# Turning the first query tile's probabilities by a DMA transpose in an attention and FFN kernel, with a reordered opening and finish

## What is computed

```python
q = rope((LN(x) @ Wq) as 32 heads of 64)
k = rope((LN(x) @ Wk) as 8 heads of 64), repeated 4 times
v = (LN(x) @ Wv) as 8 heads of 64, repeated 4 times
p = softmax(causal(q @ k.T / 8))
x = x + (p @ v) @ Wo
scale = max(absmax(LN(x)), 1e-7) / 127            # per token
xq = clip(round(LN(x) / scale), -128, 127)
x = x + float16((xq @ weight.T) * scale * w_scale + bias)
```

## Time and profile before

| | |
|---|---|
| median of three runs | 805.92 us |
| the profiled execution, its own time | 809.36 us |
| span of the profile of that execution | 807.5 us |
| PE busy | 762.0 us (94%), 8230 matmuls |
| DVE busy | 631.9 us (78%) |
| ACT busy | 627.7 us (78%) |
| POOL busy | 572.4 us (71%) |
| hardware DMA queue, share of the 16 DMA engines | 42.5% |
| chain that ended last | PE 73%, DVE 8%, ACT 5%, issue 5%, SPq 4%, DMA 4% |

### The profile page before, as it was taken

How to read it: one execution, slowest core, us unless ns; L and a number is a source line. 1 busy time by engine, 2 the same in 40 slices (tenths; PEclk the granted TensorE clock), 3 DMA queues, 4 the chain that set the end, 5 groups by cost and what they waited for, 6 DMA issues and landing times.

```text
span 807.5 us, 23412 instructions
## 1 busy us (share of the span) xinstructions
PE 762.0 (94%) x8230; PEld 641.1 (79%) x8230; DVE 631.9 (78%) x1392; ACT 627.7 (78%) x1731; POOL 572.4 (71%) x526
## 2 busy tenths in 40 slices
PE   3899999999999999999999999999999999999993
PEld 2678888888888887788888888888888887888771
DVE  5757877787878887777778888878788787887886
ACT  4488888788877887788778878888788777887772
POOL 4466877777777886877886887877786887676403
PEclk9799999999999999999999999999999999999995
DMA  8254545564554554554544454455544455354300
GB/s 263 53 124 91 132 112 139 126 153 99 133 125 99 125 122 93 122 117 108 135 114 112 100 127 112 112 125 120 125 106 116 110 117 128 80 119 100 86 2 26
DMA packets 56994, 90.99 MB, mean 113 GB/s; under 512 B 12592, under 2 KB 19248, under 8 KB 56880
## 3 DMA queue, kind: packets, MB, share of 16 engines
q1 hardware_dynamic: 53808, 79.02, 42.5%
q0 software_dynamic: 3072, 10.49, 4.9%
HBM read 16.06 MB, written 2.10 MB: 22 GB/s over the span
## 4 chain that ended last, share of the span: by engine, by line
PE 73%; DVE 8%; ACT 5%; issue 5%; SPq 4%; DMA 4%; POOL 0%; ACTq 0%; POOLq 0%; DVEq 0%
PE x_bank L623 21%; PE t_bank L735 15%; PE o_bank L751 11%; PE s_bank L719 9%; PE s_bank L720 8%; PE s_bank L722 3%; DMA qT<-wv 3%; PE ot_bank L802 3%; ACT prob L1030 2%; PE t_bank L623 2%; DVE probT L1353 2%; SPq L304 2%; SPq L338 1%; DVE o_norm L1388 1%; SPq L342 1%
## 5 line engine op out<-in xcount | busy, mean ns | idle before, releaser
L1030 ACT ACTIVATE prob<-s_bank,neg_max 128x384 f32<-128x384 f32 (+3 forms) x512 | 266.5, 531 | 62.9 <-DVE neg_max L1364 62.8
L1364 DVE TENSOR_REDUCE neg_max<-s_bank 128x1 f32<-128x384 f32 (+3 forms) x352 | 215.9, 636 | 58.3 <-PE s_bank L722 55.5
L1353 DVE SCALAR_TENSOR_TENSOR probT<-t_bank,probT 128x512 f16<-128x512 f32 x320 | 215.5, 682 | 29.5 <-ACT probT L1042 28.7
L1042 ACT ACTIVATE probT<-t_bank 128x512 f16<-128x512 f32 x320 | 189.2, 600 | 43.3 <-PE t_bank L735 38.7
L735 PE MATMUL t_bank<-ident,prob 128*128 128x128 f32 x1280 | 199.1, 278 | 5.0 <-DVE probT L1353 1.4
L719 PE MATMUL s_bank<-kT,qT 128*128 128x384 f32 (+3 forms) x512 | 178.2, 363 | 5.4 <-DMA qT<-wv 3.0
L492 POOL TENSOR_TENSOR wv<-raw,wv 128x512 fp32r<-128x512 f32 x62 | 79.6, 1284 | 132.2 <-ACT wv L991 132.2
L720 PE MATMUL s_bank<-kT,qT 128*128 128x384 f32 (+3 forms) x512 | 157.1, 322 | 0.0
L735 PEld LDWEIGHTS t_bank<-ident,prob 128*128 128x128 f32 x1280 | 137.6, 141 | 14.8 <-ACT prob L1030 7.3
L751 PE MATMUL o_bank<-value,probT 128*128 128x64 f16 x3840 | 138.4, 193 | 0.0
L751 PEld LDWEIGHTS o_bank<-value,probT 128*128 128x128 f16 x3840 | 131.4, 98 | 6.0
(11 more groups left out here) (123 smaller groups left out, 954.4 us busy)
## 6 DMA issues: line engine op xcount, KB each, us to landing
qT<-wv SPq DMA_DIRECT2D x248, 128.0 KB, 2.4
swp<-raw SPq DMA_DIRECT2D x320, 64.0 KB, 2.0
kT<-key_pair SPq DMA_DIRECT2D x128, 128.0 KB, 2.4
wg_raw<-in_w_group POOLq DMA_DIRECT2D x16, 384.0 KB, 4.8
wg_raw<-in_w_group POOLq DMA_DIRECT2D x16, 256.0 KB, 3.8
resid<-in_x SPq DMA_DIRECT2D x4, 512.0 KB, 8.7
out<-resid SPq DMA_DIRECT2D x16, 128.0 KB, 2.1
wo_stage<-in_w_out SPq DMA_DIRECT2D x4, 256.0 KB, 3.0
```

Source lines behind the costliest of these rows:

```text
L1030: nc.scalar.activation(prob[:, slot:slot + blocks, h, :], s_bank[G % SCORE_BANKS][:, at * n:(at + 1) * n].rearrange("p (k n) -> p k n", n= ...
L1042: nc.scalar.activation(turned_half[B % TURNED][HI], t_bank[B % TURN_BANKS][:, :], ACT.Copy, scale=PROB_SCALE).then_inc(probT_hi, 1)
L1353: nc.vector.scalar_tensor_tensor(out=turned_half[B % TURNED][LO], in0=t_bank[B % TURN_BANKS][:, :], scalar=PROB_SCALE, in1=turned_half[B % ...
L1364: nc.vector.tensor_reduce(neg_max[:, s % 2, u:u + len(heads)], s_bank[G % SCORE_BANKS][:, 0:len(heads) * n].rearrange("p (h n) -> p h n", ...
```

## The change

**The first query tile.** `turn(s, 0)` is gone from PE. ACT now makes the high part directly from `prob` into a new tensor `parts` (128 partitions, two parts of 4 x 128 columns in 16 bits), and DVE makes the low part from `prob` and `parts`, both in SBUF. SP then issues one DMA transpose of `parts` into `probT` (`turn_first_block`), and `attend(s, 0)` waits for that transfer. It moves from behind `turn(s, 1)` to behind `scores(s, 7)`. The split now stands at the end of the loop body before: on ACT right behind the exponentials of the first query tile, on DVE right behind `maxima(s + 1, 2)` and ahead of `add_product(s, 2)`. `invert_sums(s, 0)` and `normalise_output(s, 0)` move behind `maxima(s, 7)`. `pe_turn_no` numbers the nine turns that stay.

**Weight stage.** The output weight has one staging buffer in place of two. One chunk is loaded, rounded and subtracted in every step up to the eighth, in place of two in every second.

**Opening.** PE projects the second step's first queries ahead of `values(0)`, and `values(0)` to `values(2)` stand ahead of `turn_xn(4)`. ACT rounds the second group weight in place of POOL. DVE makes the low parts of the value weight ahead of the second batch's statistics, and `cast_ffn_weights` moves to the opening's end.

**Finish.** `normalise_output` of the last step's query tile 3 moves ahead of that step's `add_product(s, 2)`. The last four token tiles are normalised in two pairs (0 and 1, 2 and 3) in place of three and one, and tile `LOOP_TILES + 2` is normalised by ACT in place of POOL.

```diff
-WO_STAGES = 2
+WO_STAGES = 1
...
+        parts = sb("parts", [P, 2, GROUP_HEADS * P], f16)
...
+            def turn_first_block(s):
+                B = block_no(s, 0)
+                sp.wait_ge(probT_lo, B + 1)
+                if B >= TURNED:
+                    sp.wait_ge(pv_done, B - TURNED + 1)
+                sp.dma_start_transpose(probT[B % TURNED][:, :, :, :].rearrange("p a h n -> p (a h) n"),
+                                       parts[:, :, :].rearrange("p a n -> p (a n)")).then_inc(first_turned, 16)
+
             for s in range(STEPS):
+                turn_first_block(s)
                 swap_key_halves(s + 2)
...
-                if s % 2 == 0:
-                    load_wo(s + 2)
-                    load_wo(s + 3)
+                load_wo(s + 2)
...
             def attend(s, t):
...
-                pe.wait_ge(probT_lo, B + 1)
+                if t == 0:
+                    pe.wait_ge(first_turned, 16 * s + 16)
+                else:
+                    pe.wait_ge(probT_lo, B + 1)
...
             project(0, 0)
             project(0, 1)
             project_keys(0)
+            project(1, 0)
             values(0)
+            values(1)
+            values(2)
+            spread_power()
             turn_xn(4)
-            values(1)
-            spread_power()
...
             for s in range(STEPS + 1):
-                turn(s, 0)
                 scores(s, 4)
...
                 turn(s, 1)
-                attend(s, 0)
                 turn(s, 2)
                 out_product(s - 1, 3)
                 turn_quant(done_tile(s))
                 scores(s, 7)
+                attend(s, 0)
...
             def keep_probT(s, t):
...
+                if t == 0:
+                    act.wait_ge(exp_done, unit_no(s, 0, GROUP_HEADS))
+                    if s:
+                        act.wait_ge(first_turned, 16 * s)
+                    nc.scalar.activation(parts[:, HI, :], prob[:, B % PROBS, :, :].rearrange("p h n -> p (h n)"), ACT.Copy,
+                                         scale=PROB_SCALE).then_inc(probT_hi, 1)
+                    return
...
                 for h in range(GROUP_HEADS):
                     exponentials(s + 1, 0, h)
-
+                keep_probT(s + 1, 0)
...
             def keep_probT_low(s, t):
...
+                if t == 0:
+                    nc.vector.scalar_tensor_tensor(out=parts[:, LO, :], in0=prob[:, B % PROBS, :, :].rearrange("p h n -> p (h n)"),
+                                                   scalar=PROB_SCALE, in1=parts[:, HI, :],
+                                                   op0=ALU.mult, op1=ALU.subtract).then_inc(probT_lo, 1)
+                    return
...
                 maxima(s, 5)
-                keep_probT_low(s, 0)
...
-                invert_sums(s, 0)
                 keep_probT_low(s, 1)
                 add_product(s - 1, 3)
-                normalise_output(s, 0)
...
                 maxima(s, 7)
+                invert_sums(s, 0)
+                normalise_output(s, 0)
...
                 maxima(s + 1, 1)
                 maxima(s + 1, 2)
+                keep_probT_low(s + 1, 0)
+                if s == STEPS - 1:
+                    normalise_output(s, 3)
+                    aggregate(LOOP_TILES, LOOP_TILES + 2, TOK_TILES)
+                    add_eps(3, slice(LOOP_TILES, LOOP_TILES + 2))
                 add_product(s, 2)
```

166 lines of the change are left out of this document (84 added, 82 removed).

## The result

| | before | changed |
|---|---|---|
| median of four runs each | 807.34 us | 832.12 us |
| lowest to highest | 805.54 to 810.15 | 831.11 to 832.91 |
| ratio of the times, 95% interval | | 1.0303 [1.0277, 1.0329] |
| span of the profiled execution | 807.5 us | 829.7 us |

The changed kernel is 24.8 us slower, and its 832.12 us lie within the forecast range of 803 to 840 us, 4.7 us above the forecast itself. The spans differ by 22.1 us (829.66 less 807.55). The rest is the scatter of single executions.

What follows compares the result with a forecast made beforehand. The prediction took PE to bound the kernel overall, but a chain over ACT, DVE and PE at step heads. Loop 23.5, POOL 2.3, opening -3.0 and finish -1.3 made +21.5 us: 827.4 us, range 803 to 840 us.

Steps and rivals of the forecast that it cites:

- What bounds the kernel: Loop: PE is busy 248.23 of 252 us, but at step heads follows ACT and DVE, so 11.5 us saved isn't gained.
- The head of an odd step: Step 5: new copy and low part delay the chain 0.67 us, attend adds 0.35 us; the step is 1.02 us longer.
- ACT: the third exponential at 176.28: Second query tile, step 5: maxima behind DVE's low part put the fourth exponential at 176.96, 0.67 us later.
- `attend` behind the chain: Step head: attend(s, 0) leaves the chain's shadow, adding 0.35 us of PE time; turn_output(5, 0) comes at 182.39.
- The head of an even step: Step 4, where project_keys covers most of the chain: 0.09 us for the chain and 0.35 us for attend, 0.44 us longer.
- Contention with POOL: Odd steps: DVE's low part may wait for a POOL instruction; half of 0.27 us each, 2.3 us over 17 steps.
- The transfer: SP's DMA transpose lands 3.0 us after issue; attend(5, 0) has 5.5 us, 2.5 more than needed, so it costs nothing.
- The finish: Last step: normalise_output moved ahead of add_product(31, 2) removes the wait of turn_output(31, 3), gaining 1.3 us.
- The opening: Ahead of values(0): a moved projection and sooner low parts fill PE's 3.57 us wait, gaining 3.0 us, ends 0 and 3.6.
- The sum: Whole kernel: 23.5 + 2.3 - 3.0 - 1.3 = +21.5 us, giving a median of 827.4 us.
- the loop's terms: Loop: 17 heads without key projection at 1.02 us, 14 with one at 0.44, 23.5 us, plus 2.3 us for POOL.
- the odd step's own end of 0: Odd step's head: lower end of its cost, where the split costs the chain nothing; the upper end is 1.3 us.

## Why the prediction was right

**What bounds the kernel** (right). The forecast said that PE's busy share of 98.5% hides a chain over ACT, DVE and PE at the head of a step, and that 11.5 us less for PE would not arrive. The chain's rows stand where the working put them, within 0.1 us in step 5, and the turn taken back restores the median steps to within 0.04 us. With the copy where the old one stood and the low part one maximum ahead of its old place, the same kernel with all its transfers runs like the kernel before.

**The head of an odd step** (size right, one route missed). Forecast 1.02 us and 0.14 us for POOL, measured a median of 1.07 and a mean of 18.9 / 15 = 1.26 us. The step "ACT: the third exponential at 176.28" derived the 0.67 us from DVE's low part alone. The runs show two routes side by side. Without the low part 0.54 us of the 0.77 us come back, and only when ACT's copy moves as well does the chain recover, by another 0.43 us. The forecast held because the two overlap in the kernel as it is, and that is in part luck. An experiment's expectation built on DVE alone missed: 8 us in place of 11 to 15.

**`attend` behind the chain** (right for this kernel, its reason only in part). `turn_output(5, 0)` came 0.04 us from the forecast. But the 0.35 us were no free gain on offer. Put back ahead of `out_product` they met a shadow of 0.26 us and the transfer's landing, and DVE's `o_norm` was next in line.

**The head of an even step** (right): 0.44 us forecast, 0.42 measured. Over all even steps the mean is 5.5 / 15 = 0.37 us, and 0.53 us against the kernel with the turn undone. In a few steps `scores(s + 1, 0)` waits for the placing of queries, in the trace of before too (3.0 us in 6 waits), and those steps stand out of the pattern.

**Contention with POOL** (right in odd steps, left out in even ones). Half of 0.27 us was taken. Step 5 shows 0.82 - 0.69 = 0.13 us. The 32 low parts take 834 ns on average in the changed kernel, 4.6 us in all above the 0.69 us without POOL: 2.4 us in odd steps, where the forecast had 2.3, and 2.2 us in even ones, where it had none. How much of it reached the step's end isn't shown.

**The transfer** (right): 3.1 us to landing against 3.0 us forecast from an ordinary load, hidden in all 32 steps, with 2.2 us in hand against 2.5. The least in hand was 0.47 us, in step 9.

**The finish** (under-sized): 1.3 us forecast. The kernel with the turn undone shows 2.4 us from `scores(31, 0)` to the end (42.56 to 40.16 us), of which 3.80 - 2.35 = 1.45 us are the wait of the earlier trace rows.

**The opening** (size in one execution of the kind forecast, but not in this one). 3.0 us were forecast from the wait of the earlier trace rows, measured were 1.0 us. Two things took it, neither in the forecast. One is where value weights land: PE's first matmul starts at 10.26 us here and 9.90 us before. The other is the clock of the first projections. In the trace of before they ran at full speed:

```profile
13.65 1.61 PE L623 MATMUL x_bank<-xT,wg 128*128 128x512 f32 x6 [1.02 <-DVE xT L1263]
```

In the changed kernel's execution `project(0, 0)` and what follows took

```profile
14.00 2.90 PE L635 MATMUL x_bank<-xT,wg 128*128 128x512 f32 x6 [1.02 <-DVE xT L1288]
16.70 3.83 PE L635 MATMUL t_bank<-xT,wg 128*128 128x512 f32 x12
```

and in the kernel with the turn undone, which has the same opening,

```profile
12.49 1.62 PE L625 MATMUL x_bank<-xT,wg 128*128 128x512 f32 x6 [1.02 <-DVE xT L1265]
13.96 2.90 PE L625 MATMUL t_bank<-xT,wg 128*128 128x512 f32 x12
```

From PE's first matmul to `scores(0, 0)` it is 45.76 us before, 44.41 us in the changed kernel, and 51.14 - 8.75 = 42.39 us with the turn undone. So the new opening is worth 3.4 us where the first projections run at full speed, and 1.4 us where they don't. Of the nine profiled executions with this opening, three are of the first kind (42.3 to 42.4 us) and six of the second (43.7 to 45.0). There is one trace of before, so whether the half clock has to do with the new opening isn't shown. On top of it, PE's gain was partly waited away at `turn_xn(8)`, 5.03 us, in all of them.

**The sum.** Loop 25.1 us (forecast 25.8, with the last head in it), opening 1.0 (3.0), finish 2.0 with the longer last head in it (1.3): 22.1 us in the trace, 24.8 us in the medians, 21.5 forecast. Against the kernel with the turn undone the loop costs more than that, 27.4 us, and the last head another 0.4, since that kernel is itself 2.3 us shorter in the loop than the kernel before, a gain that the forecast had not. So the loop's terms were 27.8 - 25.8 = 2.0 us short, the opening 2.0 us too hopeful and the finish 1.1 us too small. With the 2.3 us this is 21.5 + 2.0 + 2.0 - 1.1 - 2.3 = 22.1 us: errors of 4.0 and 3.4 us cancel, and that the sum missed by so little is partly luck. Two terms of the loop are known to have been left out, POOL's in even steps (2.2 us on DVE) and the half clock in step 29. The range was also worked out more narrowly than the text says: its lower end for this case, 818 us, leaves out the odd step's own end of 0. Why the rest of the change gives 2.3 us in the loop wasn't followed up. Most of it falls in a few steps (10 to 12, 14, 22 and 26) at whose end the kernel before waits for placed queries: 3.0 us in all, and 0.7 us with the turn undone.

## What to carry over

Where the busiest engine waits for a chain over several engines in one stretch of a loop, taking work off it there gave nothing in this kernel, and a copy of 0.6 us put ahead of the chain cost most of its length in every round (17.7 us of loop in 31 rounds). Moving the new work back among the chain's own took one line on ACT and one on DVE and gave back 25 of the 29 us. The other 3.5 us stood in the last step alone, with PE's wait of 1.82 us for the late transfer and its lower clock behind it. Look for every route by which the moved instruction reaches the chain (here the maxima on one engine, a bank held by the other), since removing one uncovers the next. When work is to fill such a stretch, follow all that hangs on it to its last consumer first: the moved projection filled the head and then arrived too late for the next step's scores.
